# A two-layer graph network on one core: how the edge one-hots are compared

## Chip, cores and metric

The kernel runs on one core of a Trainium2 chip. The metric is the device time of one execution in microseconds. The kernel before takes 3071.88 us, the median of three runs (3070.5 to 3090.59).

## What is computed

Two graph layers over 6250 nodes of 128 features and 200000 edges, sorted by target `dst`. Cut to what matters:

```python
# layer 0
m_in  = concatenate([x[src], x[dst], edge_attr])          # 200000 x 384
m     = silu(m_in @ msg_W1 + msg_b1) @ msg_W2 + msg_b2
agg   = segment_sum(m, dst, 6250)
x     = layernorm(x + layernorm(x + mlp2(concatenate([x, agg])), gamma, beta))
# layer 1
agg   = segment_sum(x[src], dst, 6250) / max(degree, 1)
x     = layernorm(x + relu(relu(concatenate([x, agg]) @ W1 + b1) @ W2 + b2))
```

## The kernel before

The program has three parts. `build_prepare` multiplies the node table once by the source and target thirds of `msg_W1` (tables `P_d` and `Q_d` in DRAM). `build_edges` walks over all edges, and this is where the change lies. `build_nodes` updates the nodes of layer 0, forms layer 1's neighbour sums from matrices of counts (`sums_1`, PE at L1228) and updates again.

The edge part works on 56 groups of 28 tiles of 128 edges. A group is 7 quads of 4 tiles. One quad is one step of a software pipeline over the engines:

- POOL (L506 to L527) fetches the rows of `P_d` for the sources: one indirect DMA for each tile, so 4 per quad and 28 per group (L519), into `gath`. The first group's are issued in the prepare part (L241). Before a quad of group g it waits for the addition of the same quad in group g-1, which frees the buffer; it reads its row numbers from `src_i` in SBUF.
- PE (`products`, L650 and L652) multiplies the edge features by `wc` and adds the target's part by a one-hot `nodeE`, into `ps_pre`. `sums` (L682) multiplies the one-hot `edgeN` by the activated `h` into `ps_sum`, the segment sums. `count` (L666, L672) multiplies `edgeL` by `edgeK` into `ps_cnt`, the counts for layer 1.
- DVE makes the one-hots in `hots` and adds `gath` to `ps_pre` in `add` (L590). After the addition of quad s it makes the one-hots of quad s+1. Three times a group `make_keys` (L541 to L550), `expand_first` and `expand_rest` (L553, L567) prepare the next group, and `add_sums` (L597, L598) puts the group's sums away.
- ACT applies silu (L744) and copies the counts out of PSUM (L730, L736, L750).
- SP loads and stores.

All engines run their own programs in order; the semaphores between them are what orders the work. `hots` waits for `sum_mm` and `cnt_mm` (PE is through with the buffers of two quads before), then issues edgeN (L577), edgeL (L578) and four pieces of edgeK (L580), and the last one raises `onehots`, for which PE's `count` waits. `add` waits for PE's products, for the four gathers of the quad and for ACT.

A one-hot of `edgeN` says for each edge (partition) which of 128 target nodes of the group's window it belongs to: `iota` in columns is compared with the edge's number `rel_g`. `edgeL` does the same with the low seven bits of the source, `low`. `iota` is 16-bit, `rel_g` and `low` are 32-bit, `edgeN` is written in 32 bit and `edgeL` in 16 bit (bf16).

Of the kernel before, what the change touches and what calls it, by code (L numbers as in the profile page):

```python
# [19 lines left out]
ALU = mybir.AluOpType  # L20
# [4 lines left out]
P = 128  # L25
QT, GQ = 4, 7
# [382 lines left out]
def build_edges(nc, ctx, sem, sb, v):  # L409

    flag, offs, gbase, force_general = v["flag"], v["offs"], v["gbase"], v["force_general"]
    pid, ident, identb, iota, wc = v["pid"], v["ident"], v["identb"], v["iota"], v["wc"]
# [8 lines left out]
    rel_g = [sb(f"rel_g{k}", [P, GT]) for k in range(2)]  # L421
# [3 lines left out]
    low = [sb(f"low{k}", [P, GT]) for k in range(2)]  # L425
    edgeN = [sb(f"edgeN{k}", [P, QT, P]) for k in range(2)]
    edgeL = [sb(f"edgeL{k}", [P, QT, P], BF16) for k in range(2)]
# [101 lines left out]
    def vector(dve):  # L529
        v["settled"](dve)  # L530
        V = nc.vector
# [37 lines left out]
        def hots(s, q, k, first=False):  # L569

            x = (k + q) % 2
            if not first:
                dve.wait_ge(sum_mm, s - 1)
                dve.wait_ge(cnt_mm, s - 1)
            c = slice(q * QT, (q + 1) * QT)
            io = iota[:, 0:P].unsqueeze(1).broadcast_to([P, QT, P])
            V.tensor_tensor(edgeN[x][:], io, rel_g[k][:, c].unsqueeze(2).broadcast_to([P, QT, P]), ALU.is_equal)  # L577
            V.tensor_tensor(edgeL[x][:], io, low[k][:, c].unsqueeze(2).broadcast_to([P, QT, P]), ALU.is_equal)  # L578
            for j, (w0, w) in enumerate(WIN):
                last = V.tensor_scalar(edgeK[x][:, ROFF[j]:ROFF[j] + A2 * w], iota[:, w0:w0 + A2 * w],  # L580
                                       key[k][:, q * QT + j:q * QT + j + 1], None, ALU.is_equal)
            last.then_inc(onehots, 1)
# [18 lines left out]
        def group(half, k, first=False, last=False):  # L601
            g = 2 * half + k
            nxt = (half, 1) if k == 0 else (half + 1, 0)
            for q in range(GQ):
                s = g * GQ + q
                add(s, q, k, g, first and q < 2)
                if q < GQ - 1:
                    hots(s + 1, q + 1, k, first and q == 0)
                elif not last:
                    dve.wait_ge(prepared, g + 2)  # L610
                    hots(s + 1, 0, 1 - k)
                if not last and q in (2, 3, 4):
                    if q == 2:
                        make_keys(*nxt)
                    else:
                        (expand_first, expand_rest)[q - 3](*nxt, early=first)
                if q == 5 and not first:
                    add_sums(g - 1, 1 - k)

        def fast():  # L620
            for k in range(2):
                V.memset(h[k][:, :, D:D + 2], 1.0).then_inc(h_ones, 1)
            dve.sem_inc(sum_add, 1)
            make_keys(0, 0, first=True)
            expand_first(0, 0, early=True)
            expand_rest(0, 0, early=True)
            dve.wait_ge(prepared, 1)
            hots(0, 0, 0, True)
            loop(dve, lambda: group(0, 0, first=True), group, lambda: group(GROUPS // 2 - 1, 1, last=True))
            add_sums(GROUPS - 1, 1)  # L630
# [787 lines left out]
```

## Time and profile before

| | |
|---|---|
| runs | 3071.88 us median of 3 (3070.5 to 3090.59) |
| span of the profiled execution, first to last instruction | 2569.7 us |
| what lies around the span, by the median of the runs | 3071.88 - 2569.7 = 502.2 us |
| edge loop | 82 to 2094 us of the span |
| busy: PE, DVE, ACT, POOL | 2182.9, 1577.3, 847.9, 1664.2 us |
| mean granted TensorE clock | 0.919 of full speed |

The profiler gives the span of the profiled execution. Its own time, with what lies ahead of the first instruction and behind the last, is not given apart; span and surroundings together are taken as the median of the runs. "Busy" is the time in which an engine has an instruction in work; two instructions of one engine can overlap by some hundredths of a microsecond, and then busy counts the time once while the mean duration counts both. "Idle before" a group of instructions is the time in which its engine had nothing in work just ahead of them, and the releaser is what ended it; "issue" stands where the profile shows no other releaser.

### The profile page before, as it was taken

What the parts mean: (1) busy time and instruction counts of PE and PEld (TensorE: products, weight loads), DVE (VectorE), ACT (ScalarE), POOL (GpSimd) and SP (SyncE); (2) the same over time, 40 slices, a digit from 0 to 9 for tenths busy, and PEclk for the clock granted to TensorE, in tenths of its full rate; (3) what the DMA queues carried; (4) which work ended last, traced back from release to release, by engine and by line L of the source; (5) the groups of instructions that cost most, each with busy time, mean ns of one, the idle gap of its engine ahead of it and who ended that gap; (6) DMA issues with size and microseconds to landing.
All of it is one profiled execution on the core that took longest, in us unless ns stands there. A gap on an engine that the chain in (4) does not pass through costs nothing. (4 is left out here: it accounts for less than half of the span.)

```text
span 2569.7 us, 58924 instructions
## 1 busy us (share of the span) xinstructions
PE 2182.9 (85%) x21030; PEld 1871.4 (73%) x21030; DVE 1577.3 (61%) x4059; ACT 847.9 (33%) x1368; POOL 1664.2 (65%) x1618
## 2 busy tenths in 40 slices
PE   7898888888888988898889888988898878799996
PEld 7786777677777776776777776767677754699994
DVE  4786676667666766676667666766676647600005
ACT  3343333333333433333333333333333326200004
POOL 4777777777777777777777777777777755200002
PEclk9899999899899989998899999999999988899998
DMA  6555545554555555545554555455545543688871
GB/s 236 197 190 190 167 159 185 181 169 154 177 190 173 158 180 181 187 141 180 184 190 139 186 175 190 144 182 176 191 150 176 176 118 96 245 309 302 303 268 51
DMA packets 135225, 471.71 MB, mean 184 GB/s; under 512 B 55730, under 2 KB 77490, under 8 KB 113555
## 3 DMA queue, kind: packets, MB, share of 16 engines
q1 hardware_dynamic: 84586, 368.35, 41.1%
q0 software_dynamic: 50176, 102.86, 14.3%
q8 instruction: 20, 0.33, 0.0%
q14 instruction: 17, 0.14, 0.0%
q10 hardware_dynamic: 426, 0.03, 0.0%
HBM read 369.41 MB, written 101.70 MB: 183 GB/s over the span
## 5 line engine op out<-in xcount | busy, mean ns | idle before, releaser
L519 POOL DMA_INDIRECT gath<-P_d,src_i x1540 | 1543.2, 1002 | 469.4 <-issue 465.5
L650 PE MATMUL ps_pre<-wc,eT 128*128 128x128 f32 x3136 | 702.4, 306 | 13.7 <-DVE counts L567 13.7
L682 PE MATMUL ps_sum<-h,edgeN 128*128 128x129 f32 x3136 | 486.2, 302 | 265.7 <-ACT h L744 265.2
L590 DVE TENSOR_TENSOR pre<-ps_pre,gath 128x512 f32<-128x512 f32 x392 | 265.9, 678 | 588.6 <-issue 548.7
L682 PEld LDWEIGHTS ps_sum<-h,edgeN 128*128 128x128 f32 x3136 | 422.2, 209 | 278.1 <-ACT h L744 277.7
L744 ACT ACTIVATE h<-pre 128x512 f32<-128x512 f32 x392 | 247.9, 632 | 1122.2 <-DVE pre L590 1068.3
L666 PE MATMUL ps_cnt<-edgeK,edgeL 128*128 128x500 bf16 (+1 forms) x3136 | 585.1, 336 | 29.6 <-DVE edgeK L580 29.4
L580 DVE TENSOR_SCALAR edgeK<-iota,key 128x600 bf16<-128x600 f16 (+2 forms) x1568 | 526.4, 396 | 0.0
L652 PE MATMUL ps_pre<-Qw,nodeE 128*128 128x128 bf16 x4704 | 520.4, 220 | 0.0
L650 PEld LDWEIGHTS ps_pre<-wc,eT 128*128 128x128 f32 x3136 | 478.1, 192 | 32.6 <-issue 29.6
L666 PEld LDWEIGHTS ps_cnt<-edgeK,edgeL 128*128 128x128 bf16 x3136 | 320.1, 105 | 199.3 <-DVE edgeK L580 42.8
L730 ACT ACTIVATE counts<-ps_cnt 128x1000 bf16<-128x1000 f32 x392 | 404.9, 1033 | 97.5 <-PE ps_cnt L672 92.2
L652 PEld LDWEIGHTS ps_pre<-Qw,nodeE 128*128 128x128 bf16 x4704 | 399.5, 99 | 18.9
L1228 PE MATMUL ps_n<-A_c,x1h 128*128 128x120 bf16 x5488 | 294.3, 217 | 7.5 <-DVE sumT L1256 6.2
L1228 PEld LDWEIGHTS ps_n<-A_c,x1h 128*128 128x128 f16 x5488 | 291.5, 98 | 10.3 <-DVE sumT L1256 8.3
L577 DVE TENSOR_TENSOR edgeN<-iota,rel_g 128x512 f32<-128x512 f16 x392 | 267.6, 683 | 17.7 <-PE ps_sum L682 14.9
L578 DVE TENSOR_TENSOR edgeL<-iota,low 128x512 bf16<-128x512 f16 x392 | 269.0, 686 | 0.0
L1298 POOL TENSOR_TENSOR sumT<-sumT,deg 128x896 f32<-128x896 f32 x7 | 15.2, 2203 | 293.4 <-DVE sumT L1256 293.4
L1256 DVE TENSOR_TENSOR sumT<-ps_n,sumT 128x120 f32 x56 | 15.9, 283 | 273.5 <-PE ps_n L1228 273.3
L736 ACT ACTIVATE carry<-counts 128x50 bf16 x336 | 97.5, 290 | 62.9 <-ACT counts L730 62.9
L1341 ACT ACTIVATE l_hT<-u_h,l_b 128x896 f32<-128x896 f32 x7 | 7.0, 994 | 301.8 <-PE u_h L1312 301.8
L672 PEld LDWEIGHTS ps_cnt<-carry,identb 128*128 128x128 bf16 x672 | 71.7, 107 | 30.4
(128 smaller groups left out, 1021.4 us busy)
## 6 DMA issues: line engine op xcount, KB each, us to landing
eT<-eT SPq DMA_DIRECT2D x56, 1792.0 KB, 9.2
A_d<-counts SPq DMA_DIRECT2D x56, 1568.0 KB
A_c<-A_d SPq DMA_DIRECT2D x56, 1568.0 KB, 8.1
rel_b<-rel_d SPq DMA_DIRECT2D x56, 896.0 KB
gath<-P_d,src_i POOLq DMA_INDIRECT x1568
Qw<-Q_d SPq DMA_DIRECT2D x56, 96.0 KB
Q_d<-Qst SPq DMA_DIRECT2D x7, 672.0 KB, 7.8
xT_sb<-xT SPq DMA_DIRECT2D x7, 448.0 KB, 8.1
```

The lines of the kernel that those rows point to most:

```text
L519: pool.indirect_dma_start(gath[:, q, t * D:(t + 1) * D], None, v["P_d"], bass.IndirectOffsetOnAxis(ap=src_i[k][:, c:c + 1], axis=0)).then_ ...
L577: V.tensor_tensor(edgeN[x][:], io, rel_g[k][:, c].unsqueeze(2).broadcast_to([P, QT, P]), ALU.is_equal)
L578: V.tensor_tensor(edgeL[x][:], io, low[k][:, c].unsqueeze(2).broadcast_to([P, QT, P]), ALU.is_equal)
L580: last = V.tensor_scalar(edgeK[x][:, ROFF[j]:ROFF[j] + A2 * w], iota[:, w0:w0 + A2 * w], key[k][:, q * QT + j:q * QT + j + 1], None, ALU.i ...
L590: V.tensor_tensor(pre[x][:], ps_pre[x][:], gath[:, q, :], ALU.add).then_inc(pre_add, 1)
L650: T.matmul(o, eT[k][:, e0:e0 + P], wc[:], start=True, stop=False)
L652: last = T.matmul(o, nodeE[k][:, e0:e0 + P], Qw[k][:, part * D:(part + 1) * D], start=False, stop=(part == 2))
L666: last = T.matmul(o[:, :, w0:w0 + w], edgeL[x][:, j, :], r, start=(j == 0), stop=(j == QT - 1 and q == 0))
L682: last = T.matmul(ps_sum[k][:, 0:SW], edgeN[x][:, t, :], h[x][:, t, 0:SW], start=(q == 0 and t == 0), stop=(q == GQ - 1 and t == QT - 1))
L730: A.activation(counts[k][:].rearrange("p (b a) d -> p b a d", b=2)[:, :, :, bass.ds(off, W0)], ps_cnt[x][:, :, 0:AB * W0].rearrange("p b ( ...
L744: A.activation(h[x][:, :, 0:D], pre[x][:].rearrange("p (t n) -> p t n", n=D), ACT.Silu).then_inc(silu, 1)
L1228: last = nc.tensor.matmul(ps[r][:, 0:GW], x1h[:, a, part, :], A_c[r][:, a * P:a * P + GW], start=(a == 0 and part == 0), stop=(a == NB - 1 ...
```

## The change

Each of the two one-hots was made by one `tensor_tensor` compare of 4 x 128 columns, with both operands from SBUF, broadcast. Now each is made by four `tensor_scalar` compares of 128 columns, whose second operand is one column of scalars, one value per partition. The four pieces of edgeK, which were made in this form already, stay as they are. Waits and semaphores are the same.

```diff
-            c = slice(q * QT, (q + 1) * QT)
-            io = iota[:, 0:P].unsqueeze(1).broadcast_to([P, QT, P])
-            V.tensor_tensor(edgeN[x][:], io, rel_g[k][:, c].unsqueeze(2).broadcast_to([P, QT, P]), ALU.is_equal)
-            V.tensor_tensor(edgeL[x][:], io, low[k][:, c].unsqueeze(2).broadcast_to([P, QT, P]), ALU.is_equal)
+            for to, by in ((edgeN[x], rel_g[k]), (edgeL[x], low[k])):
+                for j in range(QT):
+                    V.tensor_scalar(to[:, j, :], iota[:, 0:P], by[:, q * QT + j:q * QT + j + 1], None, ALU.is_equal)
             for j, (w0, w) in enumerate(WIN):
                 last = V.tensor_scalar(edgeK[x][:, ROFF[j]:ROFF[j] + A2 * w], iota[:, w0:w0 + A2 * w],
                                        key[k][:, q * QT + j:q * QT + j + 1], None, ALU.is_equal)
```

On DVE, one quad in the middle of a group and the preparation behind it, before the change (`pre` is the addition of the gathered rows, `key` and `rel_g` are numbers of the edges):

```order
L590 TENSOR_TENSOR pre<-ps_pre,gath 128x512
L577 TENSOR_TENSOR edgeN<-iota,rel_g 128x512
L578 TENSOR_TENSOR edgeL<-iota,low 128x512
L580 TENSOR_SCALAR edgeK<-iota,key 128x1000
L580 TENSOR_SCALAR edgeK<-iota,key 128x500
L580 TENSOR_SCALAR edgeK<-iota,key 128x600 x2
L536 REGISTER_ALU
L541 TENSOR_TENSOR rel_g<-dst_i,first_i 128x28
```

And the same place of the changed kernel, where the lines of the source behind the edit are one lower:

```order
L589 TENSOR_TENSOR pre<-ps_pre,gath 128x512
L577 TENSOR_SCALAR edgeN<-iota,rel_g 128x128 x4
L577 TENSOR_SCALAR edgeL<-iota,low 128x128 x4
L579 TENSOR_SCALAR edgeK<-iota,key 128x1000
L579 TENSOR_SCALAR edgeK<-iota,key 128x500
L579 TENSOR_SCALAR edgeK<-iota,key 128x600 x2
L536 REGISTER_ALU
L541 TENSOR_TENSOR rel_g<-dst_i,first_i 128x28
```

Two instructions have become eight, in the same place between the addition and edgeK; no other instruction has moved, on DVE or on another engine.

## Rows read from the trace of the kernel before

**Rows 1.** Stages: start:end, length, busy us of PE, PEld, DVE, ACT, POOL, then clock, DMA.

```profile
82.00:2094.00 2012.00, 1720.89 (x14900) 1463.21 (x14899) 1402.08 (x3500) 737.55 (x1171) 1542.59 (x1541) 0.92 0.53 173
...
2219.00:2513.00 294.00, 286.32 (x5404) 283.84 (x5404) 20.21 (x57) 0.00 (x0) 0.63 (x1) 1.00 0.81 299
```

**Rows 2.** Who waited for whom: us in total, times, longest us.

```profile
ACT h L744 <- DVE pre L590: 1068.3, 372, 9.1
DVE pre L590 <- issue: 548.7, 161, 8.4
POOL gath L519 <- issue: 465.5, 1527, 0.3
...
PE ps_sum L682 <- ACT h L744: 265.2, 62, 6.2
...
PE ps_cnt L666 <- DVE edgeK L580: 29.4, 61, 0.7
...
POOL gath L519 <- DVE pre L590: 4.0, 13, 0.3
```

**Rows 3.** POOL's gathers: the group by line, then durations min/median/max in ns.

```profile
L519 POOL DMA_INDIRECT gath<-P_d,src_i x1540 | 1543.2, 1002 | 469.4 <-issue 465.5 <-DVE pre L590 4.0
...
L519 POOL DMA_INDIRECT gath<-P_d,src_i x1540: 940/945/3097, 82.6 to 2093.5; - x193
```

**Rows 4.** Timeline of DVE and POOL, four places: start us, length us, instruction.

```profile
163.80 1.30 DVE L580 TENSOR_SCALAR edgeK<-iota,key 128x1000 bf16<-128x1000 f16 x4
...
162.82 3.10 POOL L519 DMA_INDIRECT gath<-P_d,src_i  x1 [0.30 <-issue]
...
507.36 0.69 DVE L590 TENSOR_TENSOR pre<-ps_pre,gath 128x512 f32<-128x512 f32 x1 [1.05 <-issue]
...
507.46 0.95 POOL L519 DMA_INDIRECT gath<-P_d,src_i  x1 [0.31 <-issue]
...
508.57 0.68 DVE L578 TENSOR_TENSOR edgeL<-iota,low 128x512 bf16<-128x512 f16 x1
508.71 1.37 POOL L519 DMA_INDIRECT gath<-P_d,src_i  x1 [0.30 <-issue]
509.17 1.32 DVE L580 TENSOR_SCALAR edgeK<-iota,key 128x1000 bf16<-128x1000 f16 x4
...
529.91 2.06 POOL L519 DMA_INDIRECT gath<-P_d,src_i  x1 [0.30 <-issue]
...
531.09 1.31 DVE L580 TENSOR_SCALAR edgeK<-iota,key 128x1000 bf16<-128x1000 f16 x4
...
540.98 0.68 DVE L577 TENSOR_TENSOR edgeN<-iota,rel_g 128x512 f32<-128x512 f16 x1
541.02 1.46 POOL L519 DMA_INDIRECT gath<-P_d,src_i  x1 [0.30 <-issue]
...
541.58 0.68 DVE L578 TENSOR_TENSOR edgeL<-iota,low 128x512 bf16<-128x512 f16 x1
...
542.18 1.36 DVE L580 TENSOR_SCALAR edgeK<-iota,key 128x1000 bf16<-128x1000 f16 x4
542.78 1.00 POOL L519 DMA_INDIRECT gath<-P_d,src_i  x1 [0.30 <-issue]
```

**Rows 5.** DVE's groups by shape: busy us, mean ns, idle before and its releasers.

```profile
L590 DVE TENSOR_TENSOR pre<-ps_pre,gath 128x512 f32<-128x512 f32 x392 | 265.9, 678 | 588.6 <-issue 548.7 <-PE ps_pre L652 21.6 <-DMA gath<-P_d,src_i 17.3
L580 DVE TENSOR_SCALAR edgeK<-iota,key 128x600 bf16<-128x600 f16 x784 | 258.9, 370 | 0.0
...
L580 DVE TENSOR_SCALAR edgeK<-iota,key 128x500 bf16<-128x500 f16 x392 | 132.1, 337 | 0.0
```

**Rows 6.** Other compares with a column of scalars: durations min/median/max ns; a timeline row.

```profile
L553 DVE TENSOR_SCALAR nodeE<-rel_b,pid x112: 670/676/775, 74.2 to 2054.7; 128x1792 bf16<-128x1792 bf16 x112
...
L1165 DVE TENSOR_SCALAR x<-x,u_mv,u_rs x49: 332/339/2108, 2158.9 to 2216.3; 128x128 f32<-128x128 f32 x49
...
2211.20 1.88 DVE L1165 TENSOR_SCALAR x<-x,u_mv,u_rs 128x128 f32<-128x128 f32 x7
```

## The prediction

> **What bounds the kernel now.** I read four views, in this order. The stages first: between 82 and 2094 us the edge loop runs, and it is 2012 of the 2570 us of the span; PE is busy for 1721 us of it, DVE for 1402, POOL for 1543 [rows 1]. By busy time PE looks like the bound. The waits say otherwise [rows 2]: POOL's indirect DMAs never wait for another engine (4.0 us in all for DVE), and what stands before each is 0.3 us of "issue", 465.5 us over 1527 times; DVE's addition at L590 instead sits idle for 548.7 us, up to 8.4 us at once, ACT waits 1068 us behind it, and PE waits 265 us behind ACT. Third, POOL's own row [rows 3]: 1543.2 us busy and 469.4 us idle before are 2012.6 us, the whole stage. So POOL never stops. Its 1540 gathers (28 for each of 55 groups) follow one another at (1543.2 + 469.4) / 1540 = 1.307 us, and all others wait for what it fetches. The edge loop gets shorter only if POOL's steps do.
>
> Those steps are not all equal. The shortest gather shows 940 ns, the median 945, the mean 1002, the longest 3097 [rows 3]. The bare step is 0.944 us and 0.304 us of issue, 1.248 us. What lies above is 1543.2 - 1540 x 0.944 = 89.4 us, 0.232 us for each of the 385 quads that POOL fetches there. The fourth view, DVE beside POOL in time, shows where that comes from [rows 4]. A gather starts at 541.02, just after edgeN began at 540.98; it takes 1.46, so 0.52 more than its 0.94, and 541.02 + 0.52 = 541.54 is where edgeN makes room for edgeL (541.58). The one at 508.71 starts inside edgeL and loses 0.43: 509.14, and edgeK begins at 509.17. The one at 542.78 falls into the edgeK compares and loses 0.06. The one at 507.46 falls into the addition of L590, which has only one operand in SBUF, and loses nothing (0.95). So a gather that starts while DVE runs a compare of this kind is held until that instruction gives way, 0.03 to 0.06 us before the next one starts; I take 0.045. It can go worse: the gather at 529.91 passed by the first gap and lost 1.12, and the one at 162.82, the longest of the run, passed by all of them and lost 2.16, up to the end of edgeK.
>
> The Trainium skill (SBUF — State Buffer, Who interferes with whom) says that a two-input instruction from SBUF holds off only GpSimd's reads, and infers that it does not stall descriptor generation, while a one-source instruction in a two-port mode does. The rows at 541.02 and 508.71 contradict the first half: the two-input compares hold the gather. I follow the rows. By the page's inference the change would take away nothing and add locks; that is the third rival below, and the page gives it no number of its own.
>
> **The change, part by part.**
> 1. Removed: two compares of 512 columns per quad. edgeN starts 0.60 before edgeL and edgeL 0.60 before edgeK [rows 4], so 1.20 us of DVE per quad.
> 2. Added: eight compares of 128 columns with one column of scalars. No row shows this one. The edgeK compares have the same form: 500 columns take 337 ns in the mean, 600 take 370 [rows 5], and nodeE's 1792 take 676 in the median [rows 6]. 337 to 676 over 1292 columns is 0.262 ns a column, so 128 columns take 337 - 372 x 0.262 = 240 ns. They overlap: four edgeK compares take 1.32 us from end to end [rows 4], where their durations add to 0.47 (by the same line, for 1000 columns) + 0.337 + 0.370 + 0.370 = 1.55; each starts 0.08 before its predecessor ends. The pitch of a 16-bit one is then 0.155 us. edgeN is written in 32 bit. If that halves the rate, 0.035 more: 0.19. The ends are 0.155 (no loss) and the nearest 32-bit row, L1165 with 128 columns and two columns of scalars: seven in 1.88 us, 0.339 each in the median, pitch (1.88 - 0.34) / 6 = 0.257 [rows 6]. I take 0.19, because one scalar column fewer must be worth something and 0.19 lies between. Sum: 4 x 0.19 + 4 x 0.155 = 1.38 us for 1.20, so DVE gets 0.18 us longer per quad, 392 x 0.18 = 71 us in all (bounds: +0.04 and +0.45 per quad).
> 3. What that costs. Behind the compares on DVE stand edgeK, on which PE's count waits, and the next addition. DVE is idle 588.6 us ahead of L590 [rows 5], and PE's own wait for edgeK is 29.4 us, 61 times 0.7 at most [rows 2]. 0.18 us for each of those lies in the stretch in which PE catches up after a late gather, while POOL runs on. I cost it at 0; without that cover it is up to 71 us.
> 4. What POOL gains. An instruction of pitch p holds POOL for p - 0.045. A gather starts every 1.248 us; the mean wait over a window is the sum of squares of the holds over twice the window. Now: 2 x 0.555^2 / (2 x 1.20) = 0.257 us, times 1.20 / 1.248 gathers, is 0.247 us per quad. A gather let in at one of those two gaps comes back 1.248 us later at a fixed place: from the gap ahead of edgeL it lands in edgeK and loses 0.06 (542.78 follows 541.02 in this way), from the gap ahead of edgeK it lands past its end. That is 0.03 per quad. 0.277 x 385 = 107 us against the 89.4 measured: the model is high by 1 / 0.84.
>    After: (4 x 0.145^2 + 4 x 0.11^2) / (2 x 1.38) = 0.048, times 1.38 / 1.248, is 0.053 per quad. But the fixed step is lost: gathers now leave the new train at eight places and come back anywhere in edgeK. Its pitches, the durations less 0.08, are 0.39, 0.26, 0.29, 0.29 (1.23 together), so (0.345^2 + 0.215^2 + 2 x 0.245^2) / (2 x 1.23) = 0.116, times 1.23 / 1.248, is 0.114. Together 0.167 x 385 = 64 us, times 0.84: 54 us.
>    POOL gains 89.4 - 54 = 35 us, all of it on the path. Bounds: if edgeK stays as cheap as it is (0.03), 0.083 x 385 x 0.84 = 27, a gain of 62. If edgeN has pitch 0.257 and the model needs no discount, (4 x 0.212^2 + 4 x 0.11^2) / (2 x 1.65) = 0.069, times 1.65 / 1.248 = 0.091; with 0.114 that is 0.205 x 385 = 79, a gain of 11.
> 5. The rest is untouched: update, the 294 us of layer-1 sums bound by PE [rows 1], output.
>
> Sum: the span of 2569.7 becomes about 2535. What lies around it, 3071.88 - 2569.7 = 502.2 by the median of the runs, stays. 3071.9 - 35 = 3037 us.
>
> The Trainium skill (VectorE: DVE Perf Modes, The TRN2 errata) advises tiles of 512 elements or more, since each instruction pays a fixed cost; that speaks against the change. The trace agrees on the fixed cost (500 columns take 337 ns, 600 take 370), and the 0.18 us of part 2 holds it; but the cost falls on an engine that waits.
>
> **The rivals.**
> - A, edgeK stays in step: the gathers keep landing in harmless places. For it: the bursts of DVE start at few phases, since the landing of POOL's own gather starts many of them. Against: eight exits in place of two. Gain 62: 3010 us.
> - B, DVE's extra time is not hidden. For it: PE waits 61 times for edgeK. Against: 588.6 us of idle time ahead of L590. It decides once the catching up of a group takes longer than POOL's 28 steps. Full price 71 less the 35: 3108 us.
> - C, the two-input compares were innocent and the new ones lock: 0.053 x 385 = 20 us more, 3092 us. Against it: 541.02 and 508.71, which end where edgeN and edgeL end.
> - D, on the other side: POOL can't pass the gaps between short compares. It missed one at 529.91 and a whole train at 162.82. If the eight act as one hold of 1.335 us, the wait is 1.335^2 / (2 x 1.38) x 1.106 = 0.714 per quad, 275 us, times 0.84 is 231: 142 more than now, 3214 us. The point from which it decides: passing only every second gap, the holds are 0.335 and 0.265, and the wait with edgeK's is 0.26 per quad, 84 us, nothing gained; every fourth, 0.40 and some 129 us, slower by 40. Against it: the row at 542.78, let through inside a train of edgeK after 0.06.
>
> **How the numbers follow.** A measurement of this kernel tells about 1%, 31 us, from no change. The forecast has 0.62; its own range, gains of 11 to 62, lies on both sides of 31, and I put a little over half of it, 0.34, beyond. A has 0.15, all faster. C and a mere reshuffling of the phases have 0.12, within 1%. B has 0.04, D 0.07. Faster 0.34 + 0.15 = 0.49; same 0.28 + 0.12 + 0.01 = 0.41; slower 0.10. The range of 3008 to 3075 takes in both bounds of the forecast, and leaves out D, most of B and part of C.
>
> **What would show it.** Right: the mean of the gathers falls from 1002 to near 944 + 54 / 1.540 = 979 ns, with 0.30 of issue before each and still no wait for DVE; losses of 0.4 to 0.5 us are gone, small ones of up to 0.3 remain and fall in edgeK; edgeL's compares take about 240 ns and edgeN's 270; DVE's busy time grows although the span falls. Wrong: gathers of 1.3 to 3 us across the new train (D); POOL waiting for L589, the addition's new line, or the idle time ahead of it gone (B); a mean of 1002 or more with no loss left over long stretches of DVE (C).

## The result, and the profile after

The changed kernel takes 3121.61 us (median of 4 runs, 3117.3 to 3129.82), the kernel before 3072.57 beside it (median of 4). The ratio is 1.014, with a 95% interval from 1.0104 to 1.0175: slower by 49 us, where 3037 us was forecast and 3075 was the upper end.

Both kernels run at one of two levels, the kernel before at about 2571 us (here called the lower level) or at 3070 to 3120 us (the upper), and each series of runs kept to one level throughout, so that only kernels run beside each other are compared here.

The cores line of a profile shows that the 502.2 us that the table above puts "around the span" are not there. The changed kernel's profiled run took 3124.95 us, and its span is:

```profile
core 0: 3123.1 us, clock 0.848
```

So under 2 us lie around it. The profile of before was of the lower level (2569.7 us, clock 0.919), the runs shown with it of the upper. The kernel before, run once more with a profile and this time at the upper level, took 3086.44 us:

```profile
core 0: 3084.6 us, clock 0.854
```

That run, not the profile shown above, is what the changed kernel's profile has to be laid beside. First before, at the upper level: POOL's gathers, then the waits that differ from [rows 2].

```profile
L519 POOL DMA_INDIRECT gath<-P_d,src_i x1540 | 1580.9, 1027 | 920.6 <-issue 496.8 <-DVE pre L590 374.3 <-DMA src_i<-src_pt 49.6
...
POOL gath L519 <- DVE pre L590: 374.3, 166, 5.0
...
PE ps_sum L682 <- issue: 127.2, 202, 1.7
PE ps_pre L652 <- issue: 122.2, 217, 1.4
...
PE ps_pre L650 <- issue: 98.9, 161, 1.8
...
PE ps_cnt L666 <- issue: 65.1, 108, 1.7
...
PE ps_cnt L672 <- issue: 29.3, 46, 1.2
...
PE ps_sum L682 <- ACT h L744: 5.7, 15, 1.4
```

Then the same of the changed kernel, at the upper level too:

```profile
L519 POOL DMA_INDIRECT gath<-P_d,src_i x1540 | 1663.9, 1080 | 880.1 <-issue 513.6 <-DVE pre L589 314.7 <-DMA src_i<-src_pt 51.8
...
POOL gath L519 <- DVE pre L589: 314.7, 144, 4.7
...
PE ps_sum L681 <- issue: 202.2, 244, 2.4
...
PE ps_pre L651 <- issue: 122.5, 196, 1.7
...
PE ps_pre L649 <- issue: 101.0, 132, 17.6
PE ps_cnt L665 <- issue: 95.7, 142, 1.5
...
PE ps_cnt L671 <- issue: 12.2, 21, 1.4
```

Four things are to be seen. POOL, which never waited in [rows 3] (4.0 us), waits 374 us for DVE at the upper level: it is not the bound there. Its gathers grew by 83 us with the change (1580.9 to 1663.9), and its idle time fell by 40.5. And PE, which in [rows 2] waits for ACT and for edgeK only, now has waits "for issue": nothing that the profile shows holds it. All such rows of PE, with the small ones that are not printed, come to 457 us before and 535 after.

The fourth is that PE itself is slower between the pauses. Its busy time was 2182.9 us at the lower level and is 2474.2 at the upper (first line). One group of its products, 86 of these 291 us, shows it in the single instruction, first at the lower level (granted clock 0.919), then at the upper (0.854), with 306 and 332 ns in the mean:

```profile
PE 2474.2 (80%) x21030; PEld 2010.5 (65%) x21030; DVE 1592.8 (52%) x4059; ACT 849.4 (28%) x1368; POOL 1701.0 (55%) x1618
...
L650 PE MATMUL ps_pre<-wc,eT 128*128 128x128 f32 x3136 | 702.4, 306 | 13.7 <-DVE counts L567 13.7
...
L650 PE MATMUL ps_pre<-wc,eT 128*128 128x128 f32 x3136 | 788.6, 332 | 119.3 <-issue 98.9 <-DMA Qw<-Q_d 19.2
```

So of the 515 us between the two spans of the kernel before, 291 are longer busy time of PE, and the other 224 are more idle time: the 457 us of pauses came, and the 265 us of waiting for ACT [rows 2] went down to 5.7. Busy time and pauses together are 2931.5 of the 3084.6 us. At the upper level PE keeps the others waiting, and waits for them for 128 us in all.

What such a pause is, the timeline of PE shows, here the kernel before at the upper level, one quad's sums with pauses and the next quad's without (start us, length us, instruction, idle before):

```profile
1010.71 0.40 PE L682 MATMUL ps_sum<-h,edgeN 128*128 128x129 f32 x2 [1.08 <-issue]
...
1013.58 0.27 PE L682 MATMUL ps_sum<-h,edgeN 128*128 128x129 f32 x1 [0.96 <-issue]
1014.99 0.38 PE L682 MATMUL ps_sum<-h,edgeN 128*128 128x129 f32 x1 [1.14 <-issue]
1016.41 0.37 PE L682 MATMUL ps_sum<-h,edgeN 128*128 128x129 f32 x1 [1.05 <-issue]
...
1022.23 1.11 PE L682 MATMUL ps_sum<-h,edgeN 128*128 128x129 f32 x8
```

`sums` waits once, ahead of the first of its four products; behind that no semaphore stands between them. Yet they start 1.41 us apart (1013.58, 1014.99, 1016.41), and in the next quad the whole piece is through in 1.11 us. The changed kernel shows the same picture (1002.08, 1003.50, 1004.91, with 1.03, 1.04 and 1.04 of issue).

The changed compares themselves, in the changed kernel at the upper level (durations min/median/max in ns, then busy us and mean ns):

```profile
L577 DVE TENSOR_SCALAR edgeN<-iota,rel_g x1568: 260/280/531, 75.0 to 2648.8; 128x128 f32<-128x128 f16 x196
L577 DVE TENSOR_SCALAR edgeL<-iota,low x1568: 233/246/492, 75.8 to 2649.5; 128x128 bf16<-128x128 f16 x196
...
L577 DVE TENSOR_SCALAR edgeN<-iota,rel_g 128x128 f32<-128x128 f16 x1568 | 349.0, 294 | 220.9 <-remote 170.8 <-PE ps_sum L681 35.5 <-issue 12.1
L577 DVE TENSOR_SCALAR edgeL<-iota,low 128x128 bf16<-128x128 f16 x1568 | 309.2, 274 | 0.0
```

Medians of 280 and 246 ns, where 270 and 240 were worked out.

### The profile page after: what moved, and what is told of

It is laid out like the page before. It is cut to its first block and busy times, and to the rows that moved or that the text cites. A ratio compares the mean times of both kernels' runs of the same rounds, so it can differ in the third digit from the quotient of the medians.

```text
span 3123.1 us, 61276 instructions
## 1 busy us (share of the span) xinstructions
PE 2465.1 (79%) x21030; PEld 2004.7 (64%) x21030; DVE 1695.0 (54%) x6411; ACT 852.6 (27%) x1368; POOL 1783.8 (57%) x1618
## 5 line engine op out<-in xcount | busy, mean ns | idle before, releaser
L519 POOL DMA_INDIRECT gath<-P_d,src_i x1540 | 1663.9, 1080 | 880.1 <-issue 513.6
L649 PE MATMUL ps_pre<-wc,eT 128*128 128x128 f32 x3136 | 785.4, 331 | 102.3 <-issue 101.0
L665 PE MATMUL ps_cnt<-edgeK,edgeL 128*128 128x500 bf16 (+1 forms) x3136 | 634.4, 347 | 125.2 <-issue 95.7
L681 PE MATMUL ps_sum<-h,edgeN 128*128 128x129 f32 x3136 | 559.3, 312 | 211.0 <-issue 202.2
L651 PE MATMUL ps_pre<-Qw,nodeE 128*128 128x128 bf16 x4704 | 593.7, 233 | 126.0 <-issue 122.5
L681 PEld LDWEIGHTS ps_sum<-h,edgeN 128*128 128x128 f32 x3136 | 462.3, 215 | 249.6 <-issue 241.5
L649 PEld LDWEIGHTS ps_pre<-wc,eT 128*128 128x128 f32 x3136 | 540.1, 213 | 125.2 <-issue 120.8
L651 PEld LDWEIGHTS ps_pre<-Qw,nodeE 128*128 128x128 bf16 x4704 | 435.7, 107 | 194.7 <-issue 165.9
L577 DVE TENSOR_SCALAR edgeN<-iota,rel_g 128x128 f32<-128x128 f16 x1568 | 349.0, 294 | 220.9 <-remote 170.8
L577 DVE TENSOR_SCALAR edgeL<-iota,low 128x128 bf16<-128x128 f16 x1568 | 309.2, 274 | 0.0
```

The lines of the kernel that those rows point to most:

```text
L519: pool.indirect_dma_start(gath[:, q, t * D:(t + 1) * D], None, v["P_d"], bass.IndirectOffsetOnAxis(ap=src_i[k][:, c:c + 1], axis=0)).then_ ...
L577: V.tensor_scalar(to[:, j, :], iota[:, 0:P], by[:, q * QT + j:q * QT + j + 1], None, ALU.is_equal)
L649: T.matmul(o, eT[k][:, e0:e0 + P], wc[:], start=True, stop=False)
L651: last = T.matmul(o, nodeE[k][:, e0:e0 + P], Qw[k][:, part * D:(part + 1) * D], start=False, stop=(part == 2))
L665: last = T.matmul(o[:, :, w0:w0 + w], edgeL[x][:, j, :], r, start=(j == 0), stop=(j == QT - 1 and q == 0))
L681: last = T.matmul(ps_sum[k][:, 0:SW], edgeN[x][:, t, :], h[x][:, t, 0:SW], start=(q == 0 and t == 0), stop=(q == GQ - 1 and t == QT - 1))
```

## The experiments

They came in two sets: why the changed kernel is slower at the upper level, where it was timed, and whether the prediction's own model, which was read from a profile of the lower level, holds there.

### Before again, and the change in parts (upper level)

Before beside these: 3079.56 us.

The kernel before, unchanged:

> The kernel before, unchanged, once more with a profile. Theory A (the profiled execution of before, span 2569.7 us, was of the same kind as the timed ones, and 502 us lie around its span): span about 2570, time about 3072. Theory B (it was of another kind than the timed ones; the kernel normally takes a span of about 3070, 2 us under its time, as the changed kernel's 3123.1 for 3124.95 suggests): span about 3070, POOL waiting for the addition some 300 us, and PE with several hundred us of pauses of 0.7 and 1.4 us between instructions inside one matmul group, as after the change, and a granted clock near 0.85 instead of 0.92.

Measured: 3086.44 us, span 3084.6, a granted clock of 0.854: theory B. The rows of before at the upper level come from it; 374.3 us of waiting for DVE and 457 us of pauses are new against the profile of before that the prediction used.

Eight compares of 128 columns, but still with two inputs:

```diff
-            V.tensor_tensor(edgeN[x][:], io, rel_g[k][:, c].unsqueeze(2).broadcast_to([P, QT, P]), ALU.is_equal)
+            for j in range(QT):
+                V.tensor_tensor(edgeN[x][:, j, :], iota[:, 0:P], rel_g[k][:, q * QT + j:q * QT + j + 1].broadcast_to([P, P]), ALU.is_equal)
...
```

(edgeL in the same way.)

> edgeN and edgeL by eight two-input compares of 128 columns, same form as before, new count of instructions. Theory count (what costs is six more instructions per quad on DVE, whatever their form): as slow as the changed kernel or slower, 3120 to 3180. Theory form (what costs is the one-source form, whose operands take both ports): about as before, 3070 to 3090. Theory length (what costs is the time the two one-hots take on DVE): eight at a pitch of about 0.20 us are 1.6 us for 1.20 us, more than the changed kernel's, so 3130 to 3200.

Measured: 3128.38 us, 1.0153 [1.0125, 1.0181]. As slow as the change, with another form of compare. So what costs at this level is not the `tensor_scalar`.

One one-hot alone by four `tensor_scalar`, edgeN:

```diff
-            V.tensor_tensor(edgeN[x][:], io, rel_g[k][:, c].unsqueeze(2).broadcast_to([P, QT, P]), ALU.is_equal)
+            for j in range(QT):
+                V.tensor_scalar(edgeN[x][:, j, :], iota[:, 0:P], rel_g[k][:, q * QT + j:q * QT + j + 1], None, ALU.is_equal)
```

> Only edgeN by four one-source compares of 128 columns, edgeL as before. If the cost is spread evenly over the compares: half of the change's 49 us, about 3097. If it lies in the 32-bit output alone: 3120, else 3073.

Measured: 3107.49 us, 1.0089 [1.0065, 1.0113].

And edgeL alone, the same edit on L578:

> Only edgeL by four one-source compares of 128 columns, edgeN as before. If the cost is spread evenly: about 3097. If it lies in the 16-bit one alone: 3120, else 3073. Together with edgeN alone the two should add up to 49 us over before.

Measured: 3112.12 us, 1.0089 [1.0061, 1.0117]. Either half costs about 30 us, three more instructions a quad each, although edgeL's four are the cheaper ones. The two add up to 61 us, more than the 49 of both together.

### Number, length and engine, one at a time

Four edits that change one thing. They were first run where the kernel before takes 2571.42 us, the lower level, and so answer there, although the expectations were written for the upper one.

Six memsets of one element on DVE behind each quad's compares, with a wait that is met by then. They write a spare tile; the kernel's own work stays whole:

```diff
+            if not (first and q == 0):
+                dve.wait_ge(spared, s)
+            for j in range(6):
+                small = V.memset(spare[0:1, j:j + 1], 0.0)
+            small.then_inc(spared, 1)
```

> The kernel before, with a wait and six memsets of one element more per quad on DVE, behind the instruction on which PE waits. They take some 0.06 us each, 0.4 us together, and DVE is idle 887 us ahead of its addition in this kind of execution. Theory supply (each engine's instructions come over one path, and more of them on DVE make PE's pauses longer): +40 to +60 us, as with the six more compares. Theory chain (the compares' own length lies on the path from the addition to PE's count): behind that path, so 0 to +15 us.

Measured: 2563.07 us, 0.9966 [0.9953, 0.9979]: 8 us faster, not slower.

The same on ACT, six activations of one element behind the copy of the counts:

> The kernel before, with a wait and six activations of one element more per quad on ACT, behind the copy of the counts. Some 0.2 us each, 1.2 us per quad, and ACT is busy for less than a third of the time. Theory supply: +40 to +60 us, since it doesn't matter which engine the instructions belong to. Theory chain: silu of the next quad comes later only where ACT has no room, 0 to +30 us, and DVE's wait for its gather and products is as before.

Measured: 2569.71 us, 1.0 [0.9988, 1.0011].

No more instructions, but a longer one: edgeN is made with 80 unused columns for each of its four parts, 832 instead of 512.

```diff
-    edgeN = [sb(f"edgeN{k}", [P, QT, P]) for k in range(2)]
+    edgeN = [sb(f"edgeN{k}", [P, QT, P + 80]) for k in range(2)]
...
-            V.tensor_tensor(edgeN[x][:], io, rel_g[k][:, c].unsqueeze(2).broadcast_to([P, QT, P]), ALU.is_equal)
+            wide = iota[:, 0:P + 80].unsqueeze(1).broadcast_to([P, QT, P + 80])
+            V.tensor_tensor(edgeN[x][:], wide, rel_g[k][:, c].unsqueeze(2).broadcast_to([P, QT, P + 80]), ALU.is_equal)
```

> The kernel before, with edgeN's compare 832 columns wide instead of 512 (the 320 more are computed and not used): the same instructions, 0.33 us longer per quad, about what six more compares add in the changed kernel. Theory supply: no change, within 10 us. Theory chain: +40 to +60 us, the whole of the change's loss. If 0.33 us per quad were wholly on the path it would be 392 x 0.33 = 129 us.

Measured: 2671.08 us, 1.0382 [1.0356, 1.0408]: 100 us for 0.33 us of DVE a quad, more than either theory gave, and less than the 129 us of a length that lies wholly on the path.

Both compares left out: edgeN and edgeL are filled with zeros once, and the rest of the program runs on them, so that what is timed is the kernel without this work.

> The kernel before without the compares that make edgeN and edgeL (both are filled with zeros once, so the segment sums and counts of the output are left out in effect; PE does the same work): two instructions and 1.2 us less per quad on DVE. Theory supply: a third of the change's loss the other way, -15 us. Theory chain: 1.2 us is four times the 0.3 that the change adds, so -100 to -200 us.

Measured: 2520.38 us, 0.9809 [0.9786, 0.9831]: 51 us faster, between the two theories.

### The same kernels at the other level

At the lower level (before 2570.41 us) the changed kernel itself:

> The changed kernel again. The last four ran beside a before of 2571 us, the four before them beside one of 3080 us: one and the same kernel, two kinds of execution. Where before takes 2571 us, POOL is the bound, as the prediction read it: theory port says the gathers are held 54 us in place of 89, so 35 us less than before, 2536 (0.986), bounds 2509 to 2560; theory length (DVE's 0.3 us more per quad sets the end there too) says 1.5% more, 2610. Where before takes 3075, again 1.014 of it.

Measured: 2718.65 us, 1.0562 [1.0511, 1.0614]. Here the change costs 148 us, three times as much, and both theories missed it: the one from the prediction's own model by 183 us and with the wrong sign.

The eight two-input compares of 128 columns:

> Eight two-input compares of 128 columns again. Beside a before of 2571 us: theory port says that shorter holds help whatever the form, so below before too, by 20 to 40 us; the train is longer than with one-source compares, so a little less gain than f1. Theory form (only the one-source form lets POOL in at each gap, or only it is short enough): as before or slower. Beside a before of 3075: 1.015 again.

Measured: 2638.08 us, 1.0264 [1.0236, 1.0291]. Half of that, with the same number of instructions: at this level the form counts.

The six small memsets and the long compare again:

> Six memsets of one element more per quad on DVE, behind the compares. Beside a before of 2571 us it took 0.9966 of it and should again. Beside a before of 3075 us: theory supply (more instructions on DVE lengthen PE's pauses) says +40 to +60 us; theory chain (the compares' length lies on the path) says 0 to +15 us.

> edgeN's compare 832 columns wide in place of 512, no instruction more. Beside a before of 2571 us it took 1.038 of it and should again. Beside a before of 3075 us: theory supply says no change within 10 us, theory chain says +40 to +60 us, as much as the changed kernel's, for the same 0.33 us per quad.

Measured: 2562.87 us, 0.9968 [0.9957, 0.998], and 2668.8 us, 1.0374 [1.0355, 1.0393]. Both repeat.

At the upper level (before 3120.82 us), two compares of 256 columns for each one-hot:

```diff
+            io = iota[:, 0:P].unsqueeze(1).broadcast_to([P, 2, P])
+            for to, by in ((edgeN[x], rel_g[k]), (edgeL[x], low[k])):
+                for j in (0, 2):
+                    c = slice(q * QT + j, q * QT + j + 2)
+                    V.tensor_tensor(to[:, j:j + 2, :], io, by[:, c].unsqueeze(2).broadcast_to([P, 2, P]), ALU.is_equal)
```

> edgeN and edgeL by two two-input compares of 256 columns each. Beside a before of 2571 us: theory gaps (a gather gets in at each gap of a train of two-input compares of this length) says half the mean hold, 89 - 40 = 50 us of holds and 2531 us (0.985), faster than both kernels; theory train (more pieces, more passed gaps) says 2590 to 2620. Beside a before of 3075: two more instructions per quad, theory supply says +15 us.

Measured: 3152.8 us, 1.0106 [1.0076, 1.0136]: 32 us where 15 were expected.

edgeL alone once more:

> Only edgeL by four one-source compares of 128 columns; edgeN by the two-input one. Beside a before of 2571 us: if short one-source compares just ahead of edgeK make the gathers that arrive there pass edgeK's gaps, nearly the whole loss of the changed kernel, 2650 to 2720; if the number of pieces counts, half of it or less, 2600 to 2640. Beside a before of 3075: 1.009 again.

Measured: 3141.1 us, 1.0071 [1.0046, 1.0096].

The long compare:

> edgeN's compare 832 columns wide, no instruction more, 0.33 us longer per quad. Beside a before of 3075 us: theory supply says no change within 10 us, theory chain +40 to +60 us. Beside a before of 2571 us: 1.038 again.

Measured: 3113.88 us, 0.9984 [0.9961, 1.0008].

The six small memsets:

> A wait and six memsets of one element more per quad on DVE behind the compares. Beside a before of 3075 us: theory supply says +40 to +60 us, theory chain 0 to +15. Beside a before of 2571 us: 0.997 again.

Measured: 3135.58 us, 1.0048 [1.0029, 1.0068]: 15 us, at the end of theory chain's range and far from theory supply's.

And at the lower level (before 2571.36 us) the 256-column pieces, and the small activations on ACT:

> edgeN and edgeL by two two-input compares of 256 columns each. Beside a before of 2571 us: theory gaps says some 50 us of holds in place of 89 and 0.985 of before; theory train says 1.01 to 1.02 (half the pieces of 128 columns, which took 1.026). Beside a before of 3075 to 3120 us: 1.011 again.

> A wait and six activations of one element more per quad on ACT. Beside a before of 3075 to 3120 us: if all engines share one supply of instructions, 1.005 as with the small instructions on DVE, or more; if only DVE's count matters, 1.000 within 0.003. Beside a before of 2571 us: 1.000 again.

Measured: 2587.36 us, 1.0067 [1.0048, 1.0086], and 2571.22 us, 1.0002 [0.9992, 1.0012]. The pieces of 256 columns are not faster, as theory gaps had it. The activations have run at the lower level alone, so whether a small instruction on any engine costs at the upper one stays open.

### What follows at the lower level

The prediction's sum for POOL can now be laid beside the time. "Holds" is POOL's busy time in the row of L519 less 1540 x 0.944 = 1453.8 us; before has 89.4.

| kernel, lower level | gathers, busy us | holds | holds less 89.4 | time less before's |
|---|---|---|---|---|
| the changed kernel | 1687.9 | 234.1 | +144.7 | +148.2 |
| long edgeN | 1642.5 | 188.7 | +99.3 | +99.7 |
| long edgeN, second run | 1646.3 | 192.5 | +103.1 | +98.4 |
| eight two-input of 128 | 1616.3 | 162.5 | +73.1 | +67.7 |
| four two-input of 256 | 1557.6 | 103.8 | +14.4 | +16.0 |
| compares left out | 1490.5 | 36.7 | -52.7 | -51.0 |

The rows behind it, the changed kernel's at the lower level first:

```profile
L519 POOL DMA_INDIRECT gath<-P_d,src_i x1540 | 1687.9, 1096 | 469.3 <-issue 462.9 <-DVE pre L589 6.4
...
L519 POOL DMA_INDIRECT gath<-P_d,src_i x1540: 940/945/2753, 82.8 to 2238.7; - x193
```

The eight two-input compares of 128 columns:

```profile
L519 POOL DMA_INDIRECT gath<-P_d,src_i x1540 | 1616.3, 1050 | 469.3 <-issue 466.8 <-DVE pre L592 2.1 <-DMA src_i<-src_pt 0.3
```

The long edgeN, and below it the kernel without the two compares:

```profile
L519 POOL DMA_INDIRECT gath<-P_d,src_i x1540 | 1642.5, 1067 | 469.3 <-issue 454.4 <-DVE pre L591 14.6 <-DMA src_i<-src_pt 0.3
```

```profile
L519 POOL DMA_INDIRECT gath<-P_d,src_i x1540 | 1490.5, 968 | 470.0 <-issue 462.3 <-DVE pre L588 7.7
```

The idle time of POOL is 469 to 470 us in every one, as in [rows 3]; all that changes is how long the gathers are held, and the time follows it within 6 us in five changed kernels (one of them run twice). POOL is the bound, and the two-input compares do hold it. DVE's own length is not what counts: from the start of edgeN to the start of edgeK it is 1.20 us a quad in the kernel before, 1.44 in the changed one and 1.61 with eight two-input compares (medians), and the longest of the three trains is not the slowest kernel.

Where the changed kernel's gathers lose time is in the timeline. DVE first, at three places at the lower level:

```profile
511.21 0.75 DVE L577 TENSOR_SCALAR edgeL<-iota,low 128x128 bf16<-128x128 f16 x4
511.86 1.30 DVE L579 TENSOR_SCALAR edgeK<-iota,key 128x1000 bf16<-128x1000 f16 x4
513.08 0.67 DVE L553 TENSOR_SCALAR nodeE<-rel_b,pid 128x1792 bf16<-128x1792 bf16 x1
513.67 0.67 DVE L589 TENSOR_TENSOR pre<-ps_pre,gath 128x512 f32<-128x512 f32 x1
...
512.21 2.36 POOL L519 DMA_INDIRECT gath<-P_d,src_i  x1 [0.31 <-issue]
...
549.37 1.30 DVE L579 TENSOR_SCALAR edgeK<-iota,key 128x1000 bf16<-128x1000 f16 x4
550.59 0.67 DVE L553 TENSOR_SCALAR nodeE<-rel_b,pid 128x1792 bf16<-128x1792 bf16 x1
551.19 0.67 DVE L589 TENSOR_TENSOR pre<-ps_pre,gath 128x512 f32<-128x512 f32 x1
...
549.72 2.36 POOL L519 DMA_INDIRECT gath<-P_d,src_i  x1 [0.30 <-issue]
...
579.09 1.31 DVE L579 TENSOR_SCALAR edgeK<-iota,key 128x1000 bf16<-128x1000 f16 x4
580.31 0.69 DVE L589 TENSOR_TENSOR pre<-ps_pre,gath 128x512 f32<-128x512 f32 x1
...
579.44 1.76 POOL L519 DMA_INDIRECT gath<-P_d,src_i  x1 [0.30 <-issue]
```

The gather of 512.21 takes 2.36, so 1.42 more than its 0.94: 512.21 + 1.42 = 513.63, 0.04 before the addition begins at 513.67. It was let through neither at the three gaps inside edgeK nor ahead of nodeE. 549.72 + 1.42 = 551.14, 0.05 before 551.19; 579.44 + 0.82 = 580.26, 0.05 before 580.31. All three arrived while edgeK's first piece of 1000 columns ran, behind a train of short compares, and all three were held to the end of DVE's whole train. The longest hold in this run is 1.81 us (the 2753 ns above).

The eight two-input compares of 128 columns at the same level, same stage:

```profile
579.45 0.88 DVE L580 TENSOR_TENSOR edgeL<-iota,low 128x128 bf16<-128x128 f16 x4
580.25 1.42 DVE L582 TENSOR_SCALAR edgeK<-iota,key 128x1000 bf16<-128x1000 f16 x4
...
580.44 1.09 POOL L519 DMA_INDIRECT gath<-P_d,src_i  x1 [0.30 <-issue]
```

This gather too arrives in the 1000-column piece, loses 0.15 and is through at the first gap. Going by the start and length of each gather against DVE's instructions: in the changed kernel 152 gathers arrive in that piece and lose 130.5 us, 120 of them past three gaps or more, and those that arrive in the four edgeL compares lose 85.6 us; with two-input compares of the same width 104 arrive in the piece and lose 15.7 us. The moment of arrival does not explain it: of those that come 0.18 to 0.20 us after the piece began, all 29 in the changed kernel pass three gaps or more, and 98 of 100 with two-input compares go in at the first. So in that piece the form of the compares ahead of it makes the difference. But the two-input train is not free of passed gaps. This gather arrives in the addition, 0.09 ahead of the first of the eight:

```profile
1230.07 0.67 DVE L592 TENSOR_TENSOR pre<-ps_pre,gath 128x512 f32<-128x512 f32 x1
1230.67 0.88 DVE L578 TENSOR_TENSOR edgeN<-iota,rel_g 128x128 f32<-128x128 f16 x4
...
1233.50 0.67 DVE L592 TENSOR_TENSOR pre<-ps_pre,gath 128x512 f32<-128x512 f32 x1
...
1230.58 3.81 POOL L519 DMA_INDIRECT gath<-P_d,src_i  x1 [0.30 <-issue]
```

It loses 2.87: 1230.58 + 2.87 = 1233.45, 0.05 before the next addition, and eight compares and four pieces of edgeK have started meanwhile. The holds of each kernel at the lower level can be split by that, into gathers that went in at the first gap and gathers that passed at least one. (Counted are gathers more than 0.03 us over 0.944; a gap is passed when an instruction of DVE starts more than 0.06 us after the gather did and more than 0.02 us before the gather was let in.)

| kernel, lower level | let in at the first gap: gathers, us lost | passed one gap or more: gathers, us lost |
|---|---|---|
| before | 500, 78.0 | 9, 11.2 |
| long edgeN | 647, 172.0 | 9, 16.1 |
| four two-input of 256 | 536, 75.0 | 21, 27.9 |
| eight two-input of 128 | 398, 51.5 | 102, 111.0 |
| the changed kernel | 170, 17.9 | 211, 214.9 |
| compares left out | 268, 36.7 | 0, 0 |

Short pieces do make the ordinary holds shorter, 78.0 to 17.9 us. What they bring with them is that more gathers miss one gap or several, with two-input compares too, and twice as many with one-source ones. Why a gather misses a gap no run here shows. Elsewhere the moment of arrival may have a part in it: of the 16 gathers in the profile of before that arrive within 0.05 us after edgeN began, the eight that came 0.021 to 0.029 us after it passed a gap (2.07 us long, like the one at 529.91), and the eight that came 0.014 to 0.020 or 0.041 to 0.042 after it did not (1.46 to 1.48). In two other runs with the same compares, those with the small activations, the two kinds overlap.

### What follows at the upper level

Only kernels of one series can be compared; the first column names the series by the time of the kernel before in it. PE's pauses are the sum of all its rows "issue".

| series | kernel, upper level | DVE instructions added a quad | PE's pauses, us | gathers, busy us | ratio |
|---|---|---|---|---|---|
| 3080 | before again | 0 | 457 | 1580.9 | |
| 3080 | edgeN in four | 3 | 472 | 1590.9 | 1.0089 |
| 3080 | edgeL in four | 3 | 490 | 1559.3 | 1.0089 |
| 3080 | eight two-input of 128 | 6 | 529 | 1590.8 | 1.0153 |
| 3121 | long edgeN | 0 | 475 | 1618.5 | 0.9984 |
| 3121 | six small memsets | 6 | 501 | 1582.7 | 1.0048 |
| 3121 | edgeL in four | 3 | 512 | 1550.3 | 1.0071 |
| 3121 | four two-input of 256 | 2 | 524 | 1568.2 | 1.0106 |
| 3073 | the changed kernel | 6 | 535 | 1663.9 | 1.014 |

The long compare has gathers 38 us longer than before again (of another series) and adds 0.33 us of DVE a quad, more than the change adds, and costs nothing. So neither DVE's length nor POOL's holds are on the path at this level. The eight two-input compares hold POOL 10 us more than before and cost 49 us. What the slower kernels have in common is more instructions on DVE in the place of one, and more time in PE's pauses. The number does not set the cost: two more instructions (1.0106) cost more than six small ones (1.0048).

The pauses go with it better. In the series of 3121 the spans of the profiled runs are 27, 34 and 46 us over that of the long compare, and the pauses 26, 38 and 49 us over it. In the series of 3080 the spans are 16, 16 and 44 us over before again, and the pauses 14, 32 and 72 us; there the eight compares' PE was busy 50 us less at a granted clock of 0.864. For the changed kernel the sum closes: its span is 38.5 us over that of before again, its pauses 77 us more, PE's busy time 9 us less (2465.1) and PE's waits for others 31 us less. So within each series no kernel with longer pauses costs less than one with shorter. That compares in smaller pieces cost 0.7 to 1.5% here is measured in five kernels; that they do it through PE's pauses is the reading that fits, and no run set the pauses by themselves. The series of 3121 has no profile of before.

## Why the prediction was wrong

**"What lies around it, 502.2 by the median of the runs, stays": this step failed first.** It took a difference between two executions of different levels for a fixed piece outside the program. At the level where the kernels were timed, the span is 2 us shorter than the time, POOL waits 374 us for DVE, and PE has 457 us of pauses that the profile of before lacks. The statement "POOL never stops" was right for the profile and wrong for the runs, so the terms of part 4 did not price the timed kernel at all: 35 us of gain on POOL were forecast, and 49 us of loss measured where POOL is not the bound. The error could have been seen: no row carries 502 us, a fifth of the span, ahead of the first or behind the last instruction.

**Part 4, "how much POOL gains": the mechanism was right at the lower level, and the size and the sign were wrong.** That POOL is the bound there, that two-input compares hold its gathers, and that the time is 1540 bare steps and the holds, is what five changed kernels show within 6 us. The step that failed is the rule under both of its terms, that a gather is let in at the first gap. Forecast were 54 us of holds; measured are 234. The term for the eight compares, 0.053 us a quad or 20 us, measured 91 us (85.6 for the gathers that arrive in edgeL); the term for edgeK, 0.114 us a quad or 44 us, measured 138 us (130.5 in its first piece). The rule was no bad reading of before, where 500 of the 509 held gathers keep to it, and where 170 keep to it in the changed kernel they lose 17.9 us. What it had wrong is that the exceptions stay few: 211 gathers passed a gap after the change, for 9 before, and lost 214.9 us. The rows at 529.91 and 162.82 had shown such exceptions, and the prediction gave them to rival D with a chance of 0.07.

D's mechanism came true in part: gathers pass the gaps between short compares, but most of the loss lies in edgeK behind them, whose gaps D left open. D's sum was 142 us; at the lower level it is 148. The two agree in size and the places don't, so that is luck and not D's working confirmed. D's last step is also added up wrongly: by its own formula passing only every fourth gap gives 0.45 us a quad, 146 us of holds and a loss of 57, where 0.40, 129 and 40 stand.

The Trainium skill (SBUF — State Buffer, Who interferes with whom) says that whoever issues first gets the shared ports for the whole instruction and the other blocks. The rows at 512.21, 549.72 and 579.44 show more than that: the gather stays blocked over three or four instruction ends. The prediction says that its rows at 541.02 and 508.71 contradict the first half of this section, by which a two-input compare holds off GpSimd's reads alone. They don't: a gather reads its row numbers from `src_i` in SBUF. What they speak against is to take the section's inference, made for descriptor generation, for an indirect DMA; with the two compares left out the holds fell by 52.7 us.

**Part 1 and 2, the durations, were close.** edgeL 246 and edgeN 280 ns in the median for 240 and 270. At the lower level edgeL's four take 0.74 us from end to end in the median (0.155 x 3 + 0.24 = 0.71 was implied) and edgeN's four 0.87 (0.84), and from the start of the first to the start of edgeK the eight take 1.44 us, not 1.38. DVE gets 0.24 us longer a quad and not 0.18, inside the bounds given.

**Part 3, DVE's extra time at 0, was right in what it says, as far as shown.** At the lower level the time is used up by the holds (+145 of 148 us); DVE's idle time ahead of the addition is not gone but has grown from 588.6 to 639.9 us, and POOL waits 6.4 us for the addition in all:

```profile
L589 DVE TENSOR_TENSOR pre<-ps_pre,gath 128x512 f32<-128x512 f32 x392 | 266.8, 681 | 639.9 <-issue 508.2 <-DMA gath<-P_d,src_i 95.0 <-PE ps_pre L651 35.0
...
PE ps_cnt L665 <- DVE edgeK L579: 86.8, 112, 1.1
```

PE's wait for edgeK did grow, 29.4 [rows 2] to 86.8 us, and POOL ran on behind it. At the upper level the long compare, with more DVE time than the change adds, costs nothing (0.9984), so rival B is out there too.

**Rival C, the two-input compares innocent, fell.** At the lower level the kernel is 51 us faster without the two compares and 100 us slower with 320 more columns, and the holds changed by -52.7 and +99.3 us. Rival A, that edgeK stays in step, fell with the 234 us.

**What stays open.** What makes the pauses of PE and the lower clock, and so the two levels: the pauses stand between instructions with nothing to wait for, and one and the same program has them in some series of runs and not in others. The five series of experiments ran each on a chip of its own, so whether it is the chip or the time is not shown. Why smaller pieces on DVE cost at the upper level, and whether instructions on ACT would. And why a gather passes a gap, and more often behind short one-source compares. No version here beats the kernel before at both levels: the six small memsets gain 0.3% at the lower and lose 0.5% at the upper, and the long compare is even at the upper and loses 3.8% at the lower.

## What to carry to other kernels

Before a profile is used, lay its span beside the time of the runs; where they differ by more than a few microseconds, it is a profile of another execution, and which engine is the bound has to be read again from one that fits. Where GpSimd issues indirect DMAs back to back, count the excess of each over its shortest: that sum was the change in time within 6 us in five changed kernels, and what DVE does beside them is priced by it, not by DVE's own busy time. Count apart the gathers that missed a gap: cutting two compares into eight opened more gaps, and the gathers that used the first one lost less (18 us for 78), but 211 missed it, and all together lost 234 us instead of 89.

## What the runs showed of the hardware that was not expected

The same program takes 2571 us at a granted clock of 0.92 or 3070 to 3120 us at 0.85, one or the other through a whole series of runs, and the slower executions have some 460 to 540 us of pauses on PE, many of them between instructions of one group whose starts are then 1.41 us apart.

A gather held by DVE goes in 0.04 to 0.05 us before the next instruction starts, but not at every such gap: with eight two-input compares up to twelve were passed, 2.87 us at once, and in the changed kernel the longest hold was 1.81 us.

Six one-element instructions a quad on DVE make the kernel 8 us faster at the lower level, in both runs (0.9966 and 0.9968): the gathers' mean falls from 1002 to 996 and 999 ns.

```profile
L521 POOL DMA_INDIRECT gath<-P_d,src_i x1540 | 1533.4, 996 | 469.3 <-issue 464.5 <-DVE pre L597 4.9
```

The holds are 10 us fewer there and 4 to 5 in the second run. Both runs have one gather left that passed a gap, where before has nine with 11.2 us; that the small instructions do this by moving the moments at which gathers arrive is not shown.
